# Four rounds of routing instead of three, the first of them in half tiles beside the scans

## What is computed

```python
x = x + layernorm(attn(layernorm(x)))     # a state space layer
x = x + layernorm(ffn(layernorm(x)))      # a mixture of experts
# attn: xc, z = split(x @ W_in.T); xs = silu(conv3(xc)); dt_param(64), Bp(16), Cp(16) = split(xs @ W_x.T)
#   dt = softplus(dt_param @ W_dt.T + b_dt) + 1e-5
#   for each of 16 states n: s_t = exp(-exp(A_log[:, n]) * dt_t) * s_(t-1) + Bp_t[n] * dt_t * xs_t
#   y = (Cp @ W_C.T) * (sum of the states) + D * xs;   out = (y @ W_out.T) * silu(z)
# ffn: 8 experts (256 -> 1024 -> 256, gelu), top 2 of a softmax over x @ gate_w.T, weighted by it,
#   plus one shared expert of the same size for every token
```

## Time and profile before

| | us |
|---|---|
| median of 3 runs | 1249.29 (1247.64 to 1250.5) |
| the profiled execution | 1254.36 |
| its span, first to last instruction | 1252.6 |
| busy: PE, DVE, ACT, POOL | 1047.0, 684.6, 625.9, 704.9 |

### The profile page before, as it was taken

How to read it: one execution, slowest core, us unless ns; L and a number is a source line. 1 busy time by engine, 2 the same in 40 slices (tenths; PEclk the granted TensorE clock), 3 DMA queues, 4 the chain that set the end, 5 groups by cost and what they waited for, 6 DMA issues and landing times. The chain is left out here.

```text
span 1252.6 us, 15512 instructions
## 1 busy us (share of the span) xinstructions
PE 1047.0 (84%) x4736; PEld 833.6 (67%) x4736; DVE 684.6 (55%) x1216; ACT 625.9 (50%) x1190; POOL 704.9 (56%) x701
## 2 busy tenths in 40 slices
PE   4555588877777886897988898989999999999995
PEld 2122265655555555575877686869999999999884
DVE  1699998998987889974996350101111111111035
ACT  3784869687486685667654431212232222322234
POOL 2496968768479797588675257224343333332233
PEclk9676789898878887897989899889999999999998
DMA  6000010202002006132431595359998888897252
GB/s 181 18 29 5 34 35 18 68 1 84 1 18 68 1 21 225 43 73 59 115 80 58 183 266 152 66 157 349 335 311 269 262 279 252 257 276 221 50 177 101
DMA packets 140931, 162.68 MB, mean 130 GB/s; under 512 B 27976, under 2 KB 125984, under 8 KB 140832
## 3 DMA queue, kind: packets, MB, share of 16 engines
q1 hardware_dynamic: 124976, 142.70, 35.4%
q0 software_dynamic: 15872, 18.99, 7.9%
HBM read 135.20 MB, written 26.87 MB: 129 GB/s over the span
## 5 line engine op out<-in xcount | busy, mean ns | idle before, releaser
L1538 POOL TENSOR_TENSOR Ssum<-Ssum,S 128x512 f32<-128x512 f32 x240 | 301.3, 1270 | 84.7 <-DVE S L1151 84.0
L1013 PE MATMUL psum<-w,hT 128*128 128x256 f32 x1152 | 260.6, 384 | 5.0 <-issue 5.0
L1588 POOL DMA_INDIRECT acc_d<-y,ID x72 | 114.3, 1587 | 244.2 <-DMA acc_d<-y,ID 122.5
L1013 PEld LDWEIGHTS psum<-w,hT 128*128 128x128 f32 x1152 | 219.9, 193 | 34.8 <-issue 4.9
L1420 ACT ACTIVATE A<-dts,nea 128x512 f32<-128x512 f32 x256 | 178.0, 720 | 85.8 <-DVE S L1151 59.3
L1459 ACT ACTIVATE hT<-psum,bb 128x256 f32<-128x256 f32 x200 | 83.3, 470 | 251.3 <-PE psum L980 199.8
L980 PE MATMUL psum<-XT,w 128*128 128x256 f32 x800 | 189.9, 394 | 13.2 <-issue 10.8
L980 PEld LDWEIGHTS psum<-XT,w 128*128 128x128 f32 x800 | 156.9, 198 | 44.9 <-issue 21.8
L1127 DVE TENSOR_TENSOR psum<-us,psum 128x512 f32<-128x512 f32 x256 | 163.5, 683 | 38.6 <-PE psum L901 36.7
L1151 DVE TENSOR_TENSOR_SCAN S<-A,carry,psum 128x512 f32<-128x512 f32 x120 | 148.6, 1265 | 0.0
L1285 DVE TENSOR_TENSOR y<-bb,psum 128x256 f32<-128x256 f32 x72 | 26.9, 416 | 214.0 <-PE psum L1013 199.0
(11 more groups left out here) (150 smaller groups left out, 1318.8 us busy)
## 6 DMA issues: line engine op xcount, KB each, us to landing
w<-W SPq DMA_DIRECT2D x94, 1024.0 KB
bb<-b SPq DMA_DIRECT2D x47, 128.0 KB
xnb<-x SPq DMA_DIRECT2D x16, 256.0 KB, 2.9
Xr<-x SPq DMA_DIRECT2D x16, 256.0 KB
x_d<-gb SPq DMA_DIRECT2D x8, 512.0 KB
xn_d<-nb SPq DMA_DIRECT2D x8, 512.0 KB, 3.6
X<-x_d SPq DMA_DIRECT2D x16, 256.0 KB, 8.4
ACC<-acc_d SPq DMA_DIRECT2D x16, 256.0 KB, 6.0
```

Source lines behind the costliest of these rows:

```text
L1013: t = eng.matmul(bank(g)[:, 256 * k:256 * k + 256], hT[n % 2][:, f, 128 * k:128 * k + 128], w[:, f, :], start=f == 0, stop=f == 7)
L1538: eng.tensor_tensor(to, to, of, ALU.add).then_inc(nsum, 1)
L1588: eng.indirect_dma_start(acc_d, bass.IndirectOffsetOnAxis(ap=ID[:, col, 1:2].bitcast(u32), axis=0), y[n % NY][:, k, :], None, compute_op=A ...
```

## The change

It sets four rounds, ROUND_END = [2, 4, 6, 8]. The first chooses 8 halves (4 duos) instead of tiles, and the next three choose 5, 8 and 8 tiles; 22 halves are left for the end as before. So there are 21 tiles and 15 duos, still 36 routed groups, and 51 units instead of 47. Duos of the first round may be taken by `pairs()`; their two scatters are said four ticks apart, and scatters in general are kept in order. The ids of the last round are loaded in sets of three groups, each with a semaphore of its own. `calls` goes from 48 to 54, LATE from 6 to 5 (six shared groups at the end instead of four). `select` is rewritten in rows of 128 and has 18 operations.

In `prep` the two products with W_x (`dtc` with 80 columns, `bp` with 96) become one with 128 columns (`dbc`), whose rows hold dt and three copies of Bp in turns of 16 and then Cp; one ScalarE copy out of PSUM goes, GpSimd's first difference reads the copy that stays. W_dt is padded with zero rows to fit. `dt_sum` comes two steps later in `prep`, which may now reach k = 27. The scans of an odd chunk wait for their own carry only.

```diff
-ROUND_END = [3, 5, 8]
+ROUND_END = [2, 4, 6, 8]
+SIZE = [1, 2, 2, 2]
 NR = len(ROUND_END)
...
-TILES = [-(-(2 * TC * n - E * 255) // 256) for n in ROUND_END]
-NT = TILES[-1]
-
-NHALF = (2 * T - 256 * NT + E * 127) // 128
+CHOSEN = []
+for end, size in zip(ROUND_END, SIZE):
+    taken = sum(128 * z * n for z, n in zip(SIZE, CHOSEN))
+    sure = -(-(2 * TC * end - taken - E * (128 * size - 1)) // (128 * size))
+    CHOSEN.append(sure - sure % 2 if size == 1 else sure)
+
+NHALF = (2 * T - sum(128 * z * n for z, n in zip(SIZE, CHOSEN)) + E * 127) // 128
 NHALF += NHALF % 2
...
-FIRST_POST, LAST_POST, FIRST_PREP, LAST_PREP = 0, 27, 0, 25
-LATE = 6
+FIRST_POST, LAST_POST, FIRST_PREP, LAST_PREP = 0, 27, 0, 27
+LATE = 5
...
@@ -36,8 +45,12 @@ def routed_order():
 
 
-    order = [("t", m) for m in range(TILES[-2])]
-    tiles, duos = [("t", m) for m in range(TILES[-2], NT)], [("d", m) for m in range(NDUO)]
+    def of(r):
+        size = (SIZE + [1])[r]
+        return [("t" if size == 2 else "d", u) for u in range(FIRST[r], FIRST[r] + CHOSEN[r], 3 - size)]
+
+    order = [group for r in range(NR - 1) for group in of(r)]
+    tiles, duos = of(NR - 1), of(NR)
     while tiles or duos:
         order += tiles[:1] + duos[:1]
         tiles, duos = tiles[1:], duos[1:]
...
+SET = 3
+SETS = [[group for group in ROUTED if round_of(group) == r] for r in range(NR)]
+SETS[NR - 1:] = [SETS[-1][a:a + SET] for a in range(0, len(SETS[-1]), SET)]
+SET_OF = {group: n for n, groups in enumerate(SETS) for group in groups}
...
-        d, p, t0, t1 = (next(use) for _ in range(4))
-        say("dtc", i, d)
-        yield
-        say("bp", i, p)
-        say("dtc_out", i, d)
-        yield
-        say("bp_out", i, p)
+        d, t0, t1 = (next(use) for _ in range(3))
+        say("dbc", i, d)
+        yield
+        yield
+        say("dbc_out", i, d)
         yield
...
@@ -260,14 +279,11 @@
             elif n % 2:
                 yield
         yield
-        for m in range(TILES[r - 1] if r else 0, TILES[r]):
-            say("ids", m)
-        if r == NR - 1:
-            for m in range(NHALF):
-                say("ids", NT + m)
-        for _ in range(4):
-            yield
-        listed[0] = TILES[r] if r < NR - 1 else len(ROUTED)
+        for n in range(r, r + 1 if r < NR - 1 else len(SETS)):
+            say("ids", n)
+            for _ in range(4):
+                yield
+            listed[0] += len(SETS[n])
...
-        return (n < listed[0] and all(now[0] >= ready_at.get(key, 1 << 30)
-                                      for key in [("rows", n), ("w1", units(ROUTED[n])[0])]))
+        return n < listed[0] and all(now[0] >= ready_at.get(key, 1 << 30) for key in [("rows", n)] + [
+            ("w1", u) for u in units(ROUTED[n])[:1 if past[0] else 2]])
...
-            later(2 if direct else 5, "scatter", n)
+            at = max(2 if direct else 5, scattered[0] - now[0])
+            if groups[n][0] == "d" and not direct:
+                later(at, "scatter", n, 0, 1)
+                at += 4
+                later(at, "scatter", n, 1, 2)
+            else:
+                later(at, "scatter", n, 0, 2)
+            scattered[0] = now[0] + at
...
-                tile = ready(taken[0]) and ROUTED[taken[0]][0] == "t"
-                if tile and (not waiting_s or two):
+                routed = ready(taken[0]) and round_of(ROUTED[taken[0]]) < NR - 1
+                if routed and (not waiting_s or two):
...
-                calls = 48 if listed[0] else 26
+                calls = 54 if listed[0] else 26
...
-                elif step == "dtc":
+                elif step == "dbc":
                     i, g = a
                     ps = take(g)
                     eng.wait_ge(xs_done, 2 * i + 2)
                     if i == 0:
-                        eng.wait_ge(got_wx, 80)
+                        eng.wait_ge(got_wx, 128)
                     for k in range(2):
-                        t = eng.matmul(ps[0:80, :], wx[:, k, 0:80], xs[i % 2][:, k, :], start=k == 0, stop=k == 1)
-                    t.then_inc(full[BANK[g]], 1)
-                elif step == "bp":
-                    i, g = a
-                    ps = take(g)
-                    for k in range(2):
-                        t = eng.matmul(ps[0:96, :], wx[:, k, 80:176], xs[i % 2][:, k, :], start=k == 0, stop=k == 1)
+                        t = eng.matmul(ps, wx[:, k, :], xs[i % 2][:, k, :], start=k == 0, stop=k == 1)
                     t.then_inc(full[BANK[g]], 1)
                 elif step == "dt":
                     i, c, g = a
                     ps = take(g)
                     if c == 0:
...
                     if i % 2:
-                        if k == 0:
-                            eng.wait_ge(carried, CARRIES * (i // 2 + 1))
+                        eng.wait_ge(carried, CARRIES * (i // 2) + (k + 1 if k < 2 else 3 + (k - 2) // 4))
                         first = carry[:, k:k + 1]
                     else:
...
-                elif step == "dtc_out":
+                elif step == "dbc_out":
                     i, g = a
                     ps = evacuate(g)
                     if i >= 2:
                         eng.wait_ge(ymul, 2 * (i - 1))
-                    eng.copy(dcb[i % 2], ps[0:80, :]).then_inc(dtc_out, 1)
-                elif step == "bp_out":
-                    i, g = a
-                    ps = evacuate(g)
+                    eng.copy(dbc[i % 2], ps).then_inc(dbc_out, 1)
                     if i >= 2:
                         eng.wait_ge(mult, 32 * (i - 1))
-                    eng.copy(bp32, ps[0:96, :]).then_inc(bp_out, 1)
                     eng.copy(bst[i % 2], ps[0:96, :]).then_inc(bp_out, 1)
                 elif step == "mid_out":
                     i, = a
                     eng.wait_ge(mid, i + 1)
-                    eng.copy(bst[i % 2][0:64, :], bp32[0:64, :]).then_inc(mid_out, 1)
...
-            eng.memset(wx, 0.0).then_inc(wx_zero, 1)
...
-                    eng.wait_ge(bp_out, 2 * i + 2)
-                    eng.tensor_tensor(bp32[0:64, :], bp32[0:64, :], bst[i % 2][0:64, :], ALU.subtract).then_inc(mid, 1)
+                    eng.wait_ge(bp_out, i + 1)
+                    eng.wait_ge(xT_out, 2 * i + 2)
+                    eng.tensor_tensor(bp32, dbc[i % 2][0:64, :], bst[i % 2][0:64, :], ALU.subtract).then_inc(mid, 1)
...
                 elif step == "scatter":
-                    n, = a
+                    n, k0, k1 = a
                     eng.wait_ge(down_out, n + 1)
 
                     at, r = ROUTED.index(GROUPS[n]), round_of(GROUPS[n])
-                    if at:
+                    if at and k0 == 0:
                         wait_stored(eng, NTH[ROUTED[at - 1]])
-                    else:
+                    elif k0 == 0:
                         eng.wait_ge(acc_set, 16)
-                    if at == 0 or round_of(ROUTED[at - 1]) < r:
+                    if k0 == 0 and (at == 0 or round_of(ROUTED[at - 1]) < r):
                         for i in range(min(ROUND_END[r], LATE)):
                             for q in range(2):
                                 wait_stored(eng, NTH["s", i, q])
-                    for k, col in enumerate(columns(GROUPS[n])):
+                    for k in range(k0, k1):
+                        col = columns(GROUPS[n])[k]
                         if k and GROUPS[n][0] == "d":
...
-            eng.wait_ge(wx_zero, 1)
-            for to, fr, n in [(0, 0, 64), (64, 80, 16)] + [(80 + 32 * g, 64, 16) for g in range(3)]:
-                eng.dma_start(wx[:, :, to:to + n], wxv[:, :, fr:fr + n]).then_inc(got_wx, 16)
-            eng.dma_start(wdc[0:64, :], W_dtT).then_inc(got_v, 16)
-            eng.dma_start(wdc[64:80, :], W_CT).then_inc(got_v, 16)
+
+            for k in range(4):
+                eng.dma_start(wx[:, :, 32 * k:32 * k + 16], wxv[:, :, (80 if k == 3 else 64):][:, :, 0:16]).then_inc(got_wx, 16)
+                eng.dma_start(wx[:, :, 32 * k + 16:32 * k + 32], wxv[:, :, 16 * k:16 * k + 16]).then_inc(got_wx, 16)
+            eng.dma_start(wdt, W_dtT).then_inc(got_v, 16)
...
                 elif step == "ids":
-                    unit, = a
-                    r = UNIT_ROUND[unit]
-                    eng.wait_ge(select, SELECTED[NR if unit >= NT else r])
-                    if unit in (0, *TILES[:-1]):
-                        eng.wait_ge(tabled[r], 32 * len(ROUND[r]))
-                    row = eng.value_load(trow[0:1, unit:unit + 1], min_val=0, max_val=LROWS - (2 if unit < NT else 1))
-                    if unit < NT:
-                        eng.dma_start(ID[:, 2 * unit:2 * unit + 2, :], lists[:, bass.ds(row, 2), :]).then_inc(got_id[r], 16)
-                    else:
-                        eng.dma_start(ID[:, NT + unit, :], lists[:, bass.ds(row, 1), :].squeeze(1)).then_inc(got_id[r], 16)
+                    n, = a
+                    for unit in (u for group in SETS[n] for u in units(group)):
+                        z, r = UNITS[unit]
```

(7 more changed lines are left out.)

114 lines of the change are left out of this document (57 added, 57 removed).

## The result

Median of four runs: 1263.47 us (1263.11 to 1267.1), beside 1249.89 us (1247.64 to 1251.37) for the kernel before. The ratio is 1.0122, interval 1.0101 to 1.0143: the change makes the kernel 13.6 us slower. The forecast was 1240, the range ended at 1262.

What follows compares the result with a forecast made beforehand. DVE was taken to bound the kernel up to the last scan, PE behind it. Scans lose 24 us, the rest gains 33.5: -9.5, so the median 1249.3 becomes 1240; range 1222 to 1262 us.

Steps and rivals of the forecast that it cites:

- Which groups are through: Before the last scan 10 shared groups, 4 duos and 5 tiles, all 19, are just through; round 2's ids fall behind it.
- Behind the last scan: From last scan to span's end: 44 + 470.3 + 6 + 13.4 = 533.7 us, against 567.2 before, so 33.5 us gained.
- The hole: Stretch from the last scan's end to round 2's first up, with nothing routed listed: 44 us, between 36 and 56.
- The small pieces and the extra round: Scans: carry 4.6 us less, chunk 6 -3 without its softplus wait; one more round on DVE, +4 in chunk 2, +1 in chunk 3.
- carry: Wait of the scans for their carry, expected to take 4.6 us less, once.
- Term (a): Groups beside the scans: chunk 4 +6, chunk 5 +17, chunk 6 -3, chunk 7 +3 us.
- The slope of 0.79 us for each us of PE work: Scan time added per us of PE work, from chunk 3 (80.7 us) and chunk 6 (103.5 us) of the kernel before.
- -3 (0 if the wait only moves to the next `decay`): Chunk 6: 4 to 4.5 groups, without the 9.4 us softplus wait, -3 us; 0 if that wait only moves.
- Rival 1: Scans already PE-bound, spreads queue behind more groups in chunks 4 to 6: scans +43, result 1259 us; chance 0.24.
- point of decision: The change wins if the last scan moves by less than the 33.5 us gained after it.
- Rival 3: Scans absorb nearly all added work, +8 to +12 us, giving 1226; pointed to chunk 4's clock, 0.81, which may rise; chance 0.14.
- chunks 4 and 5 have 21 to 24 us of idle PE: Argument that the scans of these two chunks are not PE-bound already, since PE idles there 21 to 24 us.

## Why the prediction was wrong

By its own steps:

- **Which groups are through.** Right: 19 started at the last scan (10 shared, 4 duos, 5 tiles; 18.8 by the matmuls), and ids of round 2 behind it.
- **Behind the last scan.** Right in the sum, 531.9 us against 533.7, and partly by luck: the terms were off by +4.6, -3.4 and -3.0 us. The hole was 48.6 us and not 44. From the first up to PE's end (1237.30 + 13.98 = 1251.28) it was 472.85, against 470.3 + 6. PE's end to the span's end was 10.4 against 13.4. PE was busy for 471.96 of 472.90 us: the wait of 6.17 us in the earlier trace rows didn't come back, which is what the ids in sets of three were put at.
- **The small pieces and the extra round.** Near: 9.7 us gained by the first alone, of which carry and softplus were put at 4.6 and 3; 7.1 us for the round, put at 5, with 8 as its upper bound. The two errors of 2.1 us cancel. The start moved by 1.8 us, but kernels that begin alike start between 45.4 and 48.3 us, so that is no effect.
- **Term (a), the price of the groups beside the scans.** This failed. Chunks 4, 5 and 7 were put at 6 + 17 + 3 = 26 us (the 3 for tables), and the runs leave 47 for the groups, their order and the tables. The slope of 0.79 us for each us of PE work came from chunks 3 and 6 of before, with two and four groups in them; but chunk 6 also had two gelu steps where chunk 3 had one, and the slope put all of the difference down to PE. The price isn't a slope of PE's work: taking PE's work away gave 0.31 us for each us, the groups cost 7.8, 10.5 and 23 us each as the calls rise from 26 to 40, 48 and 54, and 16.7 us of the 44.4 hang on gelu steps, for which the prediction has no term.
- **Where the 21 us between 23.4 and 44.4 lie.** Chunk 6 +3.1 for -3 (6.1). The carry: its 4.6 us did go, but chunk 4 came at +7.4 with that gain in it, for +6 without it (6.0 together). Chunk 3 +3.5 for +1, chunk 5 +19.4 for +17, chunk 2 +5.5 for +4, chunk 7 +4.0 for +3 (7.4 together). The start 1.8, chunk 0 -0.3. So no chunk held the error by itself. Chunk 5 grew most, as forecast, and every chunk was a little dearer.
- **"-3 (0 if the wait only moves to the next `decay`)"** for chunk 6 named the right doubt and the wrong place. In before's order, without more groups, it is -2.8: 5.4 of the 9.4 us came back as a wait for the spread. With more groups the two waits together are as long as before, 26.8 us.
- **Rival 1** had the sign and the size, +43 for the scans and 1259 us, and its sign to look for: DVE's wait for the spreads as the first wait in chunks 4 to 6 (15.0, 23.3 and 26.8 us). Its point of decision, 33.5 us, held too. Its mechanism, scans that are bound by PE's work, is the smaller part of it: taking away 66 us of PE work gave 20.7 us, taking away the gelus, none of which is PE's, gave 41.3. PE was idle for 16 to 20 us of each of these chunks, and the one such place looked at in rows, 8.65 us, stood behind ScalarE.
- **Rival 3** had its sign, a higher clock in chunk 4 (0.81 before, 0.86 after), but not its effect.
- **What was argued against rival 1**, "chunks 4 and 5 have 21 to 24 us of idle PE", is the reading that misled. It took idle time as room. Here PE stood idle while work for it was waiting, since its list had something else next.

What stays open: why exactly the step from 48 to 54 calls is so dear. One guess: by the code, 54 calls put two calls behind 22 of the 32 scan steps, 48 put two behind 16. Two quarter steps of a group are 2 x 7.07 / 4 = 3.5 us of PE, and a scan step is 80.7 / 32 = 2.5 us, so each such place makes the next spread late, unless there are single ones between for PE to catch up. The run with half of the ups speaks against it: its quarter steps of ups are half as long, and 22.7 of the 26.8 us of wait in chunk 6 stay. What is left is the order itself, that is which steps stand before which spread and which gelu; no run moved the calls without changing their number.

## What to carry to other kernels

When work is interleaved into the lists of engines that run in order, its price is not its busy time and not a slope over a chunk. Measure the price at the density that the change will reach, find which short step on which other engine stands behind a long one (here a 0.57 us copy behind 6.31 us of gelu and table loads), and count what a wait of the bounding engine is in the chain, not under the engine whose name it has. Fill each stretch as long as a group costs less in it than it saves later (here up to 48 calls), and leave the rest for the phase where it costs its plain duration; and where a gap between two phases is left, fill it before adding work to the first.
